# Three-part bf16 maxima, scores without block-diagonal keys, and one exponential per gated unit in a four-layer decoder kernel

## The chip, the cores and the metric

The kernel runs on one core of a Trainium2 chip. The metric is the device time of one launch in microseconds (us). A core has these engines: TensorE (PE) for matmuls, VectorE (DVE), ScalarE (ACT), GpSimd (POOL), and SyncE (SP), which here only starts DMAs. Each engine runs its own instructions in program order, and semaphores join them. Matmuls write to PSUM, 8 banks of 128 x 512 f32; all else lies in SBUF, 128 partitions.

## The reference

Input x is 8 samples x 128 tokens x 128 features, with a context of the same shape. Four decoder layers follow, each of self-attention, cross-attention and a feed-forward part, each part followed by a residual sum and a layer norm. What the change touches:

```python
# L0x: keys and values of the context and of x, causal over x; 16 heads of 8
xc = concat(mem, x); q = x @ Wq; k, v = split(xc @ Wkv)
out = softmax(mask(q k^T * 8**-0.5)) v @ Wout + bout
# L1x: 16 heads of 64 over the context;  L2x: 16 heads of 8 over the context
# L3a: latent attention, rank 64, 16 heads, causal
# L3x: gated (mLSTM) stage, 8 heads of 16
cs = cumsum(log_sigmoid(f)); log_D = where(causal, cs[s] - cs[t] + i[t], -inf)
m = max_t(log_D); D = exp(log_D - m)
C = (q k^T / sqrt(16)) * D
out = C / (max(|sum_t C|, exp(-m)) + 1e-6) @ v
```

## The kernel before

Samples go in pairs (NS = 2 samples, T = 128 tokens each). Two streams, a and b, each take two pairs one after the other (a *turn* each), and every stage of a stream (L0a, L0x, L0f, L1a, L1x, L1f, L2a, L2x, L2f, L3a, L3x) is a Python generator for each engine. `TURN_ORDER` says for each engine how many steps of a and of b come next, so the streams interleave in an order fixed by hand; a stream has a ring of four PSUM banks.

An attention stage does this for each sample u (a *unit*; 8 units for a pair: two each in L0x, L1x, L2x, L3a). PE makes scores with the query token on the partition (`scores8`, `scores64`), in four banks of 4 heads. DVE takes each row's maximum over the keys (L1184; in L0x L1192 for each of two blocks and L1197 to join them) into `m_wide`, f32, 4 of each 32 columns. PE transposes it (`turn_maxima`, L479), and DVE copies the result to `mT` (`pick_maxima`, L1202). Then PE makes the scores again, transposed (`scores8_t`, L507; `scores_t`, L798 and L982), adds a causal mask (L510, L984, a bf16 identity matmul), and subtracts each head's maximum by a matmul of a constant `pick` column, broadcast, with `mT` (`less_maximum`, L492), 16 a unit and block. ACT takes one exponential of 512 columns a bank (L1743), and PE multiplies by the values (L525, L834).

Heads of 8 features sit four to a group of 32 rows. PE can work on tiles of 32 or 64 rows side by side. To take one head's product out of such a group, one side is spread to a block-diagonal form by DVE (`spread_heads`, L1177): `bd_c` (context keys), `bd_k` (own keys), `bd_q` (queries). The first scores use spread keys and `qT`, the transposed scores `bd_q` and keys.

In L3x, `units(first, second)` makes for two of four units (i = 2u + half) the scores (L1041), the mask (L1045) and the cumulated gates (L1050, `pick` with row 5 of `gates`). The other part of log D, row 2 of `gates`, is transposed (L1073), copied by ACT (L1987) and given as the bias of four exponentials a unit, one for each head (L1995). DVE multiplies (L1594). ACT makes the block-diagonal `bd_c` of x (L1974) at the start of the stage.

## Time and profile before

| | |
|---|---|
| median of 3 runs | 1021.25 us (1021.25 to 1021.33) |
| profiled execution, its own time | 1022.06 us |
| span in its profile | 1020.0 us |
| mean granted TensorE clock | 0.952 of full speed |
| PE, matmuls | 904.2 us busy, 89% |
| PE, weight loads (beside matmuls) | 700.2 us, 69% |
| DVE | 539.7 us, 53% |
| ACT | 450.7 us, 44% |
| POOL | 50.8 us, 5% |

The times come from runs without a profile, the busy times from one profiled execution. An f32 matmul of the program is two MATMUL records in the trace, each with a weight load; a bf16 one is one record. A record's duration holds some latency, so for the pace of matmuls the starts of successive groups are compared.

### The profile page before, as it was taken

Reading aid. Unit: us, or ns where it says so; the run is one execution under the profiler, and the core shown is the slowest. Engines: PE = TensorE matmul, PEld = TensorE weight load, DVE = VectorE, ACT = ScalarE, POOL = GpSimd, SP = SyncE. Lnnn points to the kernel's source line nnn. Section 1 sums busy time; section 2 is a strip of 40 time slices with the busy share of each in tenths; the row PEclk is TensorE's granted clock in tenths of the full one; section 3 lists DMA queues with packets and bytes.
Section 4 is the critical chain, followed back from the end, with each engine's and each line's share of the span. In section 5 each row is a group of like instructions: output and inputs, shape, how many; then the busy total and the mean of one; then the engine's idle time right before and its main releaser. Section 6 shows DMA issues by size and latency. Waiting matters only on the chain. (4 is left out here: it accounts for less than half of the span.)

```text
span 1020.0 us, 22561 instructions
## 1 busy us (share of the span) xinstructions
PE 904.2 (89%) x9368; PEld 700.2 (69%) x9368; DVE 539.7 (53%) x1569; ACT 450.7 (44%) x923; POOL 50.8 (5%) x71
## 2 busy tenths in 40 slices
PE   7689899999989998997987979989998989899772
PEld 5257768778778785666556757867887868686441
DVE  5733565653265575347636853655325547454345
ACT  2044343453454673574255233244465446433442
POOL 2300000010010000001000000001001000000000
PEclk8799989999999998999999999999999999999965
DMA  9100000401000301103000000040000030000000
GB/s 344 40 2 3 1 1 1 166 2 37 2 19 1 141 3 40 43 12 139 2 12 1 2 1 2 2 166 33 6 1 19 1 140 1 2 1 2 2 1 21
DMA packets 6838, 36.12 MB, mean 35 GB/s; under 512 B 721, under 2 KB 4305, under 8 KB 5458
## 3 DMA queue, kind: packets, MB, share of 16 engines
q1 hardware_dynamic: 6738, 34.68, 9.1%
q8 instruction: 76, 1.25, 0.5%
q14 instruction: 24, 0.20, 0.1%
HBM read 34.15 MB, written 0.52 MB: 34 GB/s over the span
## 5 line engine op out<-in xcount | busy, mean ns | idle before, releaser
L673 PE MATMUL bank<-xT,weights_F 128*128 128x256 f32 x832 | 202.9, 386 | 3.1 <-ACT p L1818 2.6
L673 PEld LDWEIGHTS bank<-xT,weights_F 128*128 128x128 f32 x832 | 152.0, 193 | 26.8 <-issue 4.2
L681 PEld LDWEIGHTS bank<-weights_F,p 128*128 128x128 f32 x1088 | 133.4, 191 | 18.8 <-DVE p L1363 7.2
L681 PE MATMUL bank<-weights_F,p 128*128 128x128 f32 x1088 | 141.3, 278 | 3.7 <-DVE p L1363 3.0
L1743 ACT ACTIVATE p<-bank 128x512 f32<-128x512 f32 x160 | 84.5, 601 | 121.0 <-PE bank L492 120.9
L1683 ACT ACT_TABLE_LOAD x76 | 97.5, 1283 | 12.9 <-DMA weights_con<-in_con 5.9
L1347 DVE SCALAR_TENSOR_TENSOR res<-bank,comb,res 128x128 f32<-128x128 f32 x184 | 55.7, 345 | 74.1 <-PE bank L681 71.6
L1184 DVE TENSOR_REDUCE m_wide<-bank 128x4 f32<-128x512 f32 x96 | 60.3, 684 | 43.4 <-PE bank L780 33.5
L1818 ACT ACTIVATE p<-bank 128x512 f32<-128x512 f32 x72 | 42.5, 597 | 91.6 <-PE bank L673 91.2
L1363 DVE TENSOR_TENSOR p<-p,bank 128x512 f32<-128x512 f32 x72 | 49.3, 685 | 47.5 <-PE bank L673 27.3
L1894 ACT ACTIVATE p<-bank 128x512 f32<-128x512 f32 x64 | 36.6, 598 | 51.3 <-PE bank L673 51.2
L492 PEld LDWEIGHTS bank<-mT,weights_con 32*128 32x128 f32 x1280 | 46.4, 194 | 17.4 <-issue 13.5
L492 PE MATMUL bank<-mT,weights_con 32*128 32x128 f32 x1280 | 55.1, 296 | 0.0
L1715 ACT ACTIVATE lnv<-mv,weights_con 128x2 f32<-128x2 f32 x56 | 16.6, 296 | 74.7 <-DVE mv L1139 72.7
L1192 DVE TENSOR_REDUCE mx<-bank 128x4 f32<-128x512 f32 x64 | 40.2, 682 | 16.5 <-PE bank L488 16.4
L2037 POOL TENSOR_TENSOR xb<-x_tok,biases 128x256 f32<-128x256 f32 x24 | 19.3, 806 | 575.1 <-DVE x_tok L1147 561.5
L525 PE MATMUL bank<-p,vz 128*32 128x128 f32 x1280 | 42.7, 280 | 4.5 <-ACT p L1743 4.4
L525 PEld LDWEIGHTS bank<-p,vz 128*32 128x32 f32 x1280 | 35.2, 112 | 11.0 <-issue 8.4
L525 PE MATMUL bank<-p,weights_con 128*32 128x128 f32 x1280 | 41.7, 275 | 0.0
L1207 DVE TENSOR_TENSOR attnT<-bank,res 128x128 f32<-128x128 f32 x32 | 9.3, 289 | 55.7 <-ACT res L1748 55.7
L525 PEld LDWEIGHTS bank<-p,weights_con 128*32 128x32 f32 x1280 | 35.9, 111 | 1.0
L1147 DVE TENSOR_SCALAR x_tok<-res,mv,rstd 128x128 f32<-128x128 f32 x88 | 26.4, 343 | 18.1 <-ACT rstd L1716 17.6
(319 smaller groups left out, 1356.0 us busy)
## 6 DMA issues: line engine op xcount, KB each, us to landing
weights_F<-in_L1f SPq DMA_DIRECT2D x2, 4096.0 KB, 13.8
weights_F<-in_L0f SPq DMA_DIRECT2D x2, 3456.0 KB, 13.4
weights_F<-in_L2f SPq DMA_DIRECT2D x2, 3456.0 KB, 12.1
weights_Y<-in_L1x_kv SPq DMA_DIRECT2D x2, 1024.0 KB, 10.6
weights_Z<-in_L1x SPq DMA_DIRECT2D x2, 1024.0 KB, 12.9
weights_Y<-in_L2a SPq DMA_DIRECT2D x2, 898.0 KB, 4.4
weights_Z<-in_L2x SPq DMA_DIRECT2D x2, 449.0 KB, 3.2
weights_L3m<-in_L3m SPq DMA_DIRECT2D x2, 288.0 KB, 6.1
```

The lines of the kernel that those rows point to most:

```text
L492: return mm(b[:, j * T:j * T + T], const("pick")[rows32(i), j:j + 1].to_broadcast([32, P]), s.mT[rows32(i), u], start=False, stop=last)
L525: m = mm(b[rows32(g_), cols], w, probs(g_, i), start=n == 0 and i == 0 and not (part and floor is not None), stop=n == len(blocks) - 1 and ...
L673: m = mm(b[:, k * NT:(k + 1) * NT], W[weight][:, f:f + P], s.xT[:], start=True, stop=True)
L681: m = mm(b[:, tk(u)], h[:, tk(u)], w, start=k == 0, stop=k == len(chunks) - 1)
L1184: o.count(dve.tensor_reduce(s.m_wide[:, u, 32 * i:32 * i + 4], heads(b[:], 4), X, ALU.max), free(st, "s", u, 0, i))
L1192: o.count(dve.tensor_reduce(s.mx[:, u, blk, 4 * i:4 * i + 4], heads(b[:], 4), X, ALU.max), free(st, "s", u, blk, i))
L1347: dve.scalar_tensor_tensor(r, y, s.comb[:, u, e:e + 1], r if i else s.x_tok[:, u], ALU.mult, ALU.add))
L1363: o.count(dve.tensor_tensor(s.p[:, 2 + e % 3], s.p[:, e % 2], bank(st, "up", e)[:], ALU.mult), free(st, "up", e))
L1683: act.preload_act_table_set(functions)
L1743: o.count(act.activation(s.p[:, first + i], b[:], ACT.Exp, scale=scale), free(st, "t", u, blk, i))
L1818: o.count(act.activation(s.p[:, e % 2], b[:], ACT.Silu), free(st, "gate", e))
L1894: o.count(act.activation(s.p[:, 2 * (e % 3) + half], b[:], ACT.Gelu_apprx_tanh), free("L1f", f"up{half}", e))
```

## The change

1. *Maxima in bf16.* After the four maxima of a unit, DVE splits them (`split_maxima`): copy to bf16, remainder, remainder to bf16, remainder of that, so that 12 of each 32 columns of `m_wide` hold three parts. `mT` becomes bf16, and the `pick` matmuls become bf16 with a column that sums three rows. In L1x the parts lie so that a matmul takes 64 rows (`pick64`), as the scores next to it do.
2. *No block-diagonal keys.* `scores8` uses `bd_q` (one head's columns as weights) with `keysT`, in 16 matmuls of 128 columns for 4 of 512. `bd_c` and `bd_k` and their spreads go; the spread of the queries comes before the first scores.
3. *Mask first* in `scores8_t` and in L3a's `scores_t`.
4. *L3x.* The block-diagonal form is made of the context, by POOL in L3a. Row 2 of `gates` is added by PE: a matmul with row 2 as weights and a constant `choose` column, broadcast, behind each `pick` matmul. ACT takes one exponential of 512 columns a unit.
5. *New orders* in `TURN_ORDER` for all engines.

```diff
 TURN_ORDER = {
     "pe":
-        "a1 b1 a2 b1 a2 b1 a2 b3 a1 b1 a1 b1 a1 b2 a1 b2 a3 b1 a2 b1 a1 b2 a1 b1 a1 b2 a1 b1 a1 b1 a2 b1 a6 b1 "
+        "a1 b1 a2 b1 a2 b1 a2 b3 a1 b1 a1 b3 a2 b2 a2 b1 a1 b1 a2 b1 a1 b1 a1 b1 a2 b2 a1 b1 a2 b1 a21 b1 a3 b1 "
...
+    pick_bf = sb("pick_bf", [P, 12], BF16)
-            self.mT = own("mT", NS, T)
+            self.mT = sb(f"mT_{g}", [P, NS, T], BF16)
+            self.m_part = sb(f"m_part_{g}", [P, 2, H], BF16)
...
                 def turn_maxima(st, u):
-                    if st == "L0x":
-                        pe.wait_ge(*told("maxima"))
-                    else:
-                        pe.wait_ge(*freed(st, "s", u, 0, 3))
+                    pe.wait_ge(*told("maxima"))
...
-                def scores8(st, u, keys, mask=None, blk=0):
+                def scores8(st, u, keysT, mask=None, blk=0):
-                    for i, b in enumerate(banks):
-                        filled(mm(heads(b[:], 4), s.qT[rows32(i), tk(u)], keys[rows32(i), u], start=mask is None, stop=True),
-                               st, "s", u, blk, i)
+                    for j in range(4):
+                        for i, b in enumerate(banks):
+                            m = mm(b[:, j * T:j * T + T], s.bd_q[rows32(i), u, j], keysT[rows32(i), tk(u)], start=mask is None,
+                                   stop=mask is None or j == 3)
+                            if j == 3:
+                                filled(m, st, "s", u, blk, i)
...
-                    return mm(b[:, j * T:j * T + T], const("pick")[rows32(i), j:j + 1].to_broadcast([32, P]), s.mT[rows32(i), u],
+                    return mm(b[:, j * T:j * T + T], pick_bf[rows32(i), j:j + 1].to_broadcast([32, P]), s.mT[rows32(i), u],
...
                 def scores8_t(st, u, keysT, mask=None, blk=0):
-                    for i, b in enumerate(banks):
-                        mm(heads(b[:], 4), keysT[rows32(i), tk(u)], s.bd_q[rows32(i), u], start=True, stop=False)
                     if mask is not None:
                         for b in banks:
-                            mm(heads(b[:], 4), ident_bf[:], among(mask, 4), start=False, stop=False)
+                            mm(heads(b[:], 4), ident_bf[:], among(mask, 4), start=True, stop=False)
+                    for i, b in enumerate(banks):
+                        mm(heads(b[:], 4), keysT[rows32(i), tk(u)], s.bd_q[rows32(i), u], start=mask is None, stop=False)
...
                             for n, b in enumerate(banks):
-                                m = less_maximum(u, n, b, j, True)
+                                r, at = n % 2, 4 * (n // 2) + j
+                                m = mm(b[:, j * T:j * T + T], pick_bf[rows64(r), 4 + at:5 + at].to_broadcast([64, P]),
+                                       s.mT[rows64(r), u], start=False, stop=True)
...
                             for j in range(4):
                                 h = 4 * half + j
-                                m = mm(b[:, j * T:j * T + T], const("pick")[rows32(u), h:h + 1].to_broadcast([32, P]),
-                                       s.gates[rows32(u), 5], start=False, stop=j == 3)
+                                mm(b[:, j * T:j * T + T], const("pick")[rows32(u), h:h + 1].to_broadcast([32, P]),
+                                   s.gates[rows32(u), 5], start=False, stop=False)
+                                m = mm(b[:, j * T:j * T + T], s.gates[rows32(u), 2], const("choose")[rows32(u), h:h + 1].to_broadcast([32, P]),
+                                       start=False, stop=j == 3)
...
+                def split_maxima(u):
+                    part = lambda k: heads(s.m_wide[:, u], 4)[:, :, 4 * k:4 * k + 4]
+                    done = o.count(dve.tensor_copy(heads(s.m_part[:, 0], 4), part(0)))
+                    yield
+                    dve.wait_ge(*done)
+                    done = o.count(dve.tensor_tensor(part(1), part(0), heads(s.m_part[:, 0], 4), ALU.subtract))
+                    yield
+                    dve.wait_ge(*done)
+                    done = o.count(dve.tensor_copy(heads(s.m_part[:, 1], 4), part(1)))
+                    yield
+                    dve.wait_ge(*done)
+                    o.count(dve.tensor_tensor(part(2), part(1), heads(s.m_part[:, 1], 4), ALU.subtract), sem("maxima"))
...
-                        for j in range(4):
-                            cols = slice(j * T, j * T + T)
-                            h = 40 + 4 * (i % 2) + j
-                            o.count(act.activation(s.p[:, i, cols], b[:, cols], ACT.Exp, bias=s.small[:, i // 2, h:h + 1]),
-                                    free("L3x", "D", i) if j == 3 else None)
+                        o.count(act.activation(s.p[:, i], b[:], ACT.Exp), free("L3x", "D", i))
...
                 def L3a():
+                    for u in range(NS):
+                        o.count(pool.tensor_tensor(s.bd_c[:, u], among(s.ctxT[:, tk(u)], 4), over(const("head16in64"), T), ALU.mult),
+                                sem("L3x_bd"))
```

On PE, in stream a's first L1x stage, the end of the first sample's transposed scores and the start of the second's stand so before (L798 the scores, L492 the maxima, between them stream b's L1a; the size is partitions x columns of the result, and each row is a group of program matmuls):

```order
L798 MATMUL bank<-wide 128x128 x4
L492 MATMUL bank<-mT,weights_con 128x128 x4
L441 MATMUL bank<-weights_con,x_tok 128x128 x2
L715 MATMUL bank<-xT,weights_L1a 32x128 x2
L719 MATMUL bank<-weights_L1a,xT 128x256 x2
L464 MATMUL bank<-weights_L1a,xT 128x128 x2
L798 MATMUL bank<-wide 128x128 x4
L492 MATMUL bank<-mT,weights_con 128x128 x4
```

and so in the changed kernel, where L800 are the same scores and L805 the maxima:

```order
L800 MATMUL bank<-wide 128x128 x4
L805 MATMUL bank<-mT,pick_bf 128x128 x4
L446 MATMUL bank<-weights_con,x_tok 128x128 x2
L717 MATMUL bank<-xT,weights_L1a 32x128 x2
L721 MATMUL bank<-weights_L1a,xT 128x256 x2
L469 MATMUL bank<-weights_L1a,xT 128x128 x2
L800 MATMUL bank<-wide 128x128 x4
L805 MATMUL bank<-mT,pick_bf 128x128 x4
```

Nothing moved here; what changed is the type and the 64 rows of L805's operands, which the sizes do not show, so that four matmuls of each kind still alternate.

On DVE, the first maxima of stream a's and b's first L0x stage, before (L1192 the maxima of a block, L1197 their join, L1177 the spreads, L1202 the copy of the transpose):

```order
L1192 TENSOR_REDUCE mx<-bank 128x4 x4
L1197 TENSOR_TENSOR m_wide<-mx 128x4x4
L1177 TENSOR_TENSOR wide<-wide,weights_con 128x512 x2
L1202 COPY mT<-bank 128x128
L1177 TENSOR_TENSOR wide<-qk,weights_con 128x512 x2
L1192 TENSOR_REDUCE mx<-bank 128x4 x4
L1172 COPY vz<-bank 128x16x8 x2
L1177 TENSOR_TENSOR wide<-qk,weights_con 128x512 x2
```

and changed (L1216, L1221, L1183 and L1229 are the same operations, L1188 to L1197 the split):

```order
L1216 TENSOR_REDUCE mx<-bank 128x4 x4
L1221 TENSOR_TENSOR m_wide<-mx 128x4x4
L1188 CAST m_part<-m_wide 128x16
L1191 TENSOR_TENSOR m_wide<-m_wide,m_part 128x4x4
L1194 CAST m_part<-m_wide 128x16
L1197 TENSOR_TENSOR m_wide<-m_wide,m_part 128x4x4
L1178 COPY vz<-bank 128x16x8 x2
L1229 CAST mT<-bank 128x128
L1183 TENSOR_TENSOR wide<-qk,weights_con 128x512 x2
```

Before, the transpose could follow L1197 at once and the spreads stood between; now four small operations stand before the transpose, and the spreads of the queries (L1183) come ahead of the scores.

On PE, stream a's last L3x stage, before (L1073 the transposes of `gates`, L1041 scores, L1045 mask, L1050 `pick`; L458, L1026 and L441 are stream b's, which ends its L3a):

```order
L1073 MATMUL bank<-weights_con,wide 128x64 x2
L1041 MATMUL bank<-wide,ctxT 128x512 x2
L1045 MATMUL bank<-neg_causal_t_bf,ident_bf 128x512 x2
L1050 MATMUL bank<-wide,weights_con 128x128 x8
L458 MATMUL bank<-weights_L3a,attnT 128x128 x2
L1026 MATMUL bank<-ctxT,weights_L3x 32x128 x4
L441 MATMUL bank<-weights_con,x_tok 128x128 x2
```

and changed (L463 and L1030 are stream b's L458 and L1026, L1080 the transpose, L1046 scores, L1051 mask, L1056 `pick`, L1058 `choose`):

```order
L463 MATMUL bank<-weights_L3a,attnT 128x128 x2
L1030 MATMUL bank<-ctxT,weights_L3x 32x128 x4
L1080 MATMUL bank<-weights_con,wide 128x64
L1046 MATMUL bank<-xT,wide 128x128 x8
L1051 MATMUL bank<-neg_causal_t_bf,ident_bf 128x512 x2
L1056 MATMUL bank<-wide,weights_con 128x128
L1058 MATMUL bank<-weights_con,wide 128x128
```

The scores are eight matmuls for two, and the last two rows come eight times in a call, one `choose` behind each `pick`; stream b's `project`, which stood behind the call, is ahead of it.

## Rows read from the trace of the kernel before

**Rows 1.** the page, part 1: busy us, share of the span, instructions

```profile
span 1020.0 us, 22561 instructions
PE 904.2 (89%) x9368; PEld 700.2 (69%) x9368; DVE 539.7 (53%) x1569; ACT 450.7 (44%) x923; POOL 50.8 (5%) x71
```

**Rows 2.** three stretches, PE alone: length, busy (count), granted clock, DMA share, GB/s

```profile
110.00:380.00 270.00, 254.85 (x2448) 0.99 0.09 35
380.00:620.00 240.00, 208.98 (x2451) 0.96 0.07 27
950.00:1020.00 70.00, 39.75 (x382) 0.69 0.03 9
```

**Rows 3.** PE's waits: us in total, times, longest us

```profile
PE bank L479 <- DVE m_wide L1197: 3.3, 3, 1.6
PE bank L507 <- DVE mT L1202: 3.8, 5, 1.7
PE bank L488 <- DVE mT L1202: 2.4, 3, 1.5
PE bank L982 <- DVE mT L1202: 1.4, 3, 0.5
```

**Rows 4.** timeline of PE, 96 to 100 us: start us, us, what, [idle before]

```profile
96.49 1.14 PE L507 MATMUL bank<-wide,qk 32*128 32x512 f32 x8
97.56 1.04 PE L510 MATMUL bank<-neg_causal_t_bf,ident_bf 128*128 128x512 bf16 x4
98.53 1.17 PE L492 MATMUL bank<-mT,weights_con 32*128 32x128 f32 x32
99.64 1.16 PE L681 MATMUL bank<-weights_F,p 128*128 128x128 f32 x8
```

**Rows 5.** timeline of PE, 567 to 570 us

```profile
567.26 1.89 PE L673 MATMUL bank<-xT,weights_F 128*128 128x256 f32 x8
568.99 1.03 PE L486 MATMUL bank<-neg_causal_bf,ident_bf 128*128 128x512 bf16 x4
569.95 1.13 PE L488 MATMUL bank<-wide,qk 32*128 32x512 f32 x7
```

**Rows 6.** timeline of PE, one sample of an L1x unit

```profile
190.62 0.71 PE L798 MATMUL bank<-wide 64*128 64x128 f32 x8
191.26 0.50 PE L492 MATMUL bank<-mT,weights_con 32*128 32x128 f32 x8
191.69 0.72 PE L798 MATMUL bank<-wide 64*128 64x128 f32 x8
...
194.93 0.27 PE L726 MATMUL bank<-weights_con,wide 64*128 64x64 f32 x1
```

**Rows 7.** timeline of PE in stage L3x, 450 us

```profile
450.35 1.71 PE L1050 MATMUL bank<-wide,weights_con 32*128 32x128 f32 x16
451.98 1.16 PE L681 MATMUL bank<-weights_F,p 128*128 128x128 f32 x8
```

**Rows 8.** timeline of PE, router logits with 8 moving columns

```profile
299.95 0.51 PE L666 MATMUL bank<-weights_small,xT 128*128 128x8 f32 x4
300.31 1.54 PE L673 MATMUL bank<-xT,weights_F 128*128 128x256 f32 x6
```

**Rows 9.** timeline of DVE, 998 us: small operations that each wait for the last

```profile
998.19 0.17 DVE L1609 TENSOR_SCALAR small<-small 128x16 f32<-128x16 f32 x1
998.39 0.25 DVE L1610 RECIPROCAL small<-small 128x16 f32<-128x16 f32 x1
```

**Rows 10.** groups of DVE by form: busy us, mean ns

```profile
L1177 DVE TENSOR_TENSOR wide<-qk,weights_con 128x512 f32<-128x512 f32 x32 | 22.1, 730 | 0.0
```

**Rows 11.** groups of POOL by form

```profile
L2066 POOL TENSOR_TENSOR x_all<-weights_L3m 128x512 f32<-128x512 f32 x1 | 1.3, 1260 | 0.0
```

**Rows 12.** groups of ACT by form

```profile
L1743 ACT ACTIVATE p<-bank 128x512 f32<-128x512 f32 x160 | 84.5, 601 | 121.0 <-PE bank L492 120.9
L1995 ACT ACTIVATE p<-bank,small 128x128 f32<-128x128 f32 x64 | 17.4, 382 | 18.8 <-PE bank L1050 18.8
```

More of the change, by code:

```diff
@@ L50 @@
                ("ones", 128), ("spread", 128), ("tiny16", 128), ("feats", 64), ("head8in32", 4), ("head16in64", 4),
-               ("pick", 8), ("cos", 8), ("sin", 8), ("eps", 5)]:
+               ("pick", 8), ("choose", 8), ("pick3", 4), ("pick64", 8), ("cos", 8), ("sin", 8), ("eps", 5)]:
     CONST[_n] = (_at, _w)
@@ L531, in probs_at, with softmax8 @@
                     return lambda g_, i: s.p[:, first + g_, i * T:i * T + T]
-                def softmax8(st, keys, keysT):
-                    scores8(st, 0, keys)
+                def softmax8(st, keysT):
+                    pe.wait_ge(*told("queries", NS))
+                    scores8(st, 0, keysT)
                     yield
@@ L945, in L2x @@
                     pe.wait_ge(*freed("L2x", "q"))
-                    pe.wait_ge(*told("L2x_keys", NS))
-                    yield from softmax8("L2x", s.bd_k, s.kT)
+                    pe.wait_ge(*freed("L2x", "k"))
+                    yield from softmax8("L2x", s.kT)
                     project("L2x", W["L2x_o"])
@@ L1071, in L3x @@
                     pe.wait_ge(*told("L3x_gates"))
-                    for k, row in enumerate((4, 2)):
-                        m = tr(b[:, 64 * k:64 * k + 64], s.gates[:, row], IDENT[0:64, 0:64])
-                    filled(m, "L3x", "mx")
+                    filled(tr(b[:, 0:64], s.gates[:, 4], IDENT[0:64, 0:64]), "L3x", "mx")
                     yield
-                    pe.wait_ge(*told("L3x_bd"))
+                    pe.wait_ge(*told("L3x_bd", NS))
                     units(0, 3)
@@ L1183, in maxima @@
                         b = bank(st, "s", u, 0, i)
-                        o.count(dve.tensor_reduce(s.m_wide[:, u, 32 * i:32 * i + 4], heads(b[:], 4), X, ALU.max),
+                        at = 32 * (2 * (i % 2) + i // 2 if st == "L1x" else i)
+                        o.count(dve.tensor_reduce(s.m_wide[:, u, at:at + 4], heads(b[:], 4), X, ALU.max),
                                 free(st, "s", u, 0, i))
+                    yield
+                    dve.wait_ge(*freed(st, "s", u, 0, 3))
+                    yield from split_maxima(u)
                 def block_maxima(st, u, blk):
@@ L1214, in softmax @@
                     yield
-                    if queries is not None:
-                        spread_heads(s.bd_q, queries, sem("queries"))
-                        yield
                     yield from maxima(st, 1)
@@ L1261, in L0a @@
                         dve.wait_ge(*told("kept"))
-                    def context_keys():
-                        dve.wait_ge(*freed("L0x", "kc"))
-                        spread_heads(s.bd_c, s.kcT, sem("L0x_ctx_keys"))
-                    yield from tail("L0a", s.x_in, context_keys)
+                    yield from tail("L0a", s.x_in)
                 def L0x():
@@ L1546, in L2x @@
                     dve.wait_ge(*freed("L2x", "q"))
+                    spread_heads(s.bd_q, s.qT, sem("queries"))
                     yield
-                    yield from softmax("L2x", s.qT)
+                    yield from softmax("L2x")
                     for u in range(NS):
@@ L1971, in L3x @@
                     exp_ln()
-                    act.wait_ge(*ring.freed((pair, "L3a", "xT")))
-                    for j in range(4):
-                        o.count(act.activation(s.bd_c[:, :, j], by_sample(s.xT[:]), ACT.Identity,
-                                               scale=const("head16in64")[:, j:j + 1]), sem("L3x_bd") if j == 3 else None)
-                    yield
                     act.wait_ge(*told("L3x_absf"))
@@ L1984, in L3x @@
                     b = bank("L3x", "mx")
-                    per_head = lambda k: b[:, 64 * k:64 * k + 64].rearrange("p (u h) -> p u h", u=NS)[:, :, 0:HC]
-                    o.count(act.activation(s.small[:, :, 32:40], per_head(0), ACT.Exp, scale=-1.0))
-                    link(act.copy(s.small[:, :, 40:48], per_head(1)), free("L3x", "mx"))
+                    per_head = b[:, 0:64].rearrange("p (u h) -> p u h", u=NS)[:, :, 0:HC]
+                    o.count(act.activation(s.small[:, :, 32:40], per_head, ACT.Exp, scale=-1.0), free("L3x", "mx"))
                     yield
```

69 lines of the change are left out of this document (35 added, 34 removed), and 55 rows, old and new, of the table TURN_ORDER.

## The prediction, before the changed kernel was run

> **What bounds the kernel now.** I read the page's part 1 first: TensorE (PE) is busy 904.2 of 1020.0 us, DVE and ACT about half of it, POOL 5% [rows 1]. So PE work is the first suspect, and the question is where it is gap-free. The windows answer that [rows 2]. From 110 to 380 us, where one stream is in an expert stage (L0f, L1f) and the other in L1a or L1x, PE is busy 254.85 of 270 us, 94%. From 380 to 620 us, where the streams pass through L3a, L3x, L0a and L0x, it is 209 of 240 us, 87%. In the last 70 us it is 40. PE time taken out of the first stretch (and of its twin in the second turn) should come off the end nearly whole; in the second, part of it turns into waiting; in the last, a chain of waits rules and not PE's work. The waits show what would be late there: PE waits for the maxima, as DVE makes them (L1197) or copies them (mT, L1202), 14 times in four rows, for 10.9 us [rows 3], out of 32 units (8 for each of 4 pairs) that go through such a chain.
>
> **How PE's time is made up.** An end is modelled, so I take starts. An f32 matmul is two records. Eight records of 256 columns start 1.73 us before the next group, 0.216 each, 0.84 ns a column; four bf16 records of 512 columns take 0.96 us, or 0.86 without one change of tile shape, 0.42 ns a column [rows 5]. So f32 costs four bf16 passes. Thirty-two records of 32 rows run on four row groups at a time: 8 x 128 x 0.84 = 0.86 us, and the row says 1.11 to the next group; the same for 4 x 512 columns is 1.07 [rows 4]. The 0.2 to 0.25 over is what a change of tile shape costs. L1x shows it best: 8 records of 64 rows take 0.65 us before 32-row ones start, where 4 x 128 x 0.84 = 0.43 is streaming, and those take 0.43 where 0.215 is [rows 6]. Each change costs 0.22 us, and a unit has eight: 194.93 - 190.62 = 4.31 us.
>
> **The change on PE.**
> (a) *bf16 maxima outside L1x.* There are 40 groups of 16 maxima matmuls, 8 of them in L1x. For the other 32, 16 bf16 matmuls on four row groups stream for 4 x 128 x 0.42 = 0.215 us instead of 0.86, with the shape change kept: -0.65 us each, -20.8 us. Bounds: the load of weights may set the pace instead. Four f32 records with 8 moving columns take 0.36 us [rows 8], 0.09 each, so a load alone can take as long as 107 ns of f32 streaming. If a bf16 load is no faster, four row groups side by side give 4 x 0.107 = 0.43 us, and the gain is 13.9. I take the streaming value, since four f32 pairs of load and matmul already pass in 0.107 us here, with half of these loads gone in bf16.
> (b) *L1x, maxima as 64-row tiles.* The alternation stays, but the shape no longer changes: 4 x (0.43 + 0.107) + one change = 2.36 us for 4.31, -1.95 x 8 = -15.6 us. With loads at 0.107: 4 x (0.43 + 0.215) + 0.22 = 2.8, -12.1. If f32 to bf16 on one shape cost as a shape change does, it would be -3.4; but [rows 5] has f32 to bf16 at 128 rows with 1.73 for 8 x 0.216, so nothing is paid there.
> (c) *Mask first in L0x's transposed scores.* 32, 128, 32 rows becomes 128, 32, 32: one change less in 8 groups, -1.8. In L3a it is 128, 64, 32 for 64, 128, 32: nothing.
> (d) *Scores against kT, 16 x 128 columns for 4 x 512 in 24 groups.* Same columns; 1.11 for 1.07 [rows 4], +1.0. L3x's scores likewise keep their columns, and rotate over the same two row groups: 0.
> (e) *L3x, the bias by PE.* A call of units() has 8 pick matmuls, the four of a unit on one row group, so nothing runs beside them: 451.98 - 450.35 = 1.63 us [rows 7]. The change puts a choose matmul of the same size and row group behind each: +1.63 x 8 = +13.1 us at full clock, twice that at half. Gone are 4 small transposes, -0.4.
> Sum on PE: -20.8 - 15.6 - 1.8 + 1.0 + 13.1 - 0.4 = -24.5 us.
>
> **The change elsewhere.** DVE: four small operations for each of 32 units, each waiting for the one before, at 0.20 us from start to start [rows 9]: 0.8 us longer from the last reduction to the transpose, +26 us of DVE in all. In return 24 spreads (L1177) go, 0.73 us each [rows 10], -17.5. DVE's total hardly moves, and half of it is idle. What is queued behind the four on DVE is the other stream's work; who waits for them is PE at its next transpose. With the 14 waits above and 0.8 us each, the most that is exposed is 11 us as the waits now stand; against it the spreads of keys in L0x go. I take +3 (four units). The first scores of L0x and L2x used to start from qT itself; now they wait for the spread of the queries, two operations or 1.5 us later, and PE's queue behind them with them: eight such places, 12 us if nothing covered them. What covers them is the other stream's matmuls, which stand ahead of the scores in PE's order; I take +2. ACT: in L3x four exponentials of 128 columns, 2.18 us a call for 8, become one of 512 a unit, 0.60 [rows 12]: -1.0 us a call. That shortens the chain in the last 70 us by two to four calls, and the doubled PE work, there partly at 1.2 for 2.4 GHz (0.69 granted, [rows 2]), lengthens it by as much; I set the two against each other. POOL makes the block-diagonal context, two operations of 128x512 a pair at about 1.26 us [rows 11], at the start of L3a for reads in L3x; without that cover a pair would wait 2.5 us. ACT gets two more table loads in the new order (82 for 80); it is not the bound, 0.
> The part of (a) in stages with 87% cover (24 groups, 15.6 us) I count at 85%: +2.4.
> Sum: -24.5 + 3 + 2 + 2.4 = **-17 us**. The profiled execution took 1022.06 (span 1020.0 and 2 around it), the median is 1021.25; I expect about 1005 profiled and **1004 us** median, 1000 to 1008 with small errors of the terms.
>
> Of loads, the Trainium skill ("TensorE: Matmul & The Clock Gate", LDWEIGHTS) says that a load takes its columns over 1.2 GHz, 107 ns for 128, whatever the rows; its section on weight-path modes says that non-f32 weights of 128 columns load about twice as fast. [Rows 8] has 0.09 us a load and agrees roughly for f32. By the first rule alone (a) and (b) would be the lower values, by the second the upper ones.
>
> **Rivals.**
> *Loads set the pace:* -13.9 - 12.1 - 1.8 + 1.0 + 13.1 - 0.4 + 7.4 = -7, 1014 us. For it: [rows 8]. Against: half as many loads per matmul. 0.15.
> *The split maxima bind (slower):* the four operations are queued in order on DVE, and a 0.7 us reduction of the other stream can stand between any two. If each of the 32 units is exposed for the 0.8 us and one such operation, 1.5 us, that is 48 us against 24.5: 1021 + 24 = 1045. It decides from 24.5/32 = 0.77 us a unit on. Against it: only 14 of 32 units are waited for now, and in the 94% stretches PE has expert matmuls in between. At its threshold it is a draw, a little above it 1025 to 1030. 0.07; the draw itself, within 0.2%, 0.03.
> *The clock falls more often:* the granted clock is 0.96 from 380 to 620 us and 0.99 from 110 to 380 [rows 2]; a share 1 - c of lost clock costs at most that share of the stretch, 9.6 and 2.7 us, 15 over the kernel. If lighter PE groups doubled it: 1019. 0.07. The same page of the Trainium skill (HAM oscillation) ties half clock to idle stretches; by it, L3x with doubled matmuls would rather gain clock, as its PE queue has fewer gaps.
> *The new orders also close waits:* PE's idle time is 116 us [rows 1]; 31 of it stand between 380 and 620 us, 17 more than 94% cover would leave [rows 2]. If the orders take 10 to 15 of these: 989 to 994. 0.18.
> My forecast: 0.50.
>
> **Range and chances.** Low end 988, by the last rival; high end 1014, by the load rival. The slower rival, the draw and the clock's stay out (0.17), with what lies under 988. Faster by over 0.2% (what a measurement of this kernel tells from no change) 0.90, within 0.2% 0.03, slower 0.07.
>
> **What would show it.** (1) Maxima groups: half the records; 0.46 us to the next group where the shape changes (0.68 if loads pace). (2) An L1x unit 2.4 us for 4.3. (3) L3x: 3.3 us a call at full clock. (4) PE busy near 880; idle near 116 to 125. (5) PE waits for the last of the four small operations, in fewer than 20 of 32 units. The prediction is wrong if PE's busy time falls as said and its idle time takes it back, or if the matmuls of (1) and (2) don't get shorter.

## The result and the profile after

| | us, median | range, runs | ratio to before, 95% interval |
|---|---|---|---|
| before | 1021.25 | 1019.62 to 1026.75, 6 | |
| changed | 1048.61 | 1043.46 to 1051.67, 6 | 1.0254 [1.0219, 1.0288] |

The changed kernel is 27 us slower, where 17 us faster was forecast. The page of its profiled execution (1047.02 us, span 1045.0) begins so; it answers to [rows 1]:

```profile
span 1045.0 us, 22918 instructions
PE 908.7 (87%) x9524; PEld 725.5 (69%) x9524; DVE 550.3 (53%) x1674; ACT 439.9 (42%) x857; POOL 55.5 (5%) x79
```

PE's busy time did not fall to 880 but rose by 4.5, and its idle time rose from 115.9 to 136.3. Yet the products that the change makes cheaper became so. The timeline of PE in the changed kernel at the maxima of one unit, and in L1x (one sample of a unit), answers to [rows 4] and [rows 6]:

```profile
419.77 0.39 PE L497 MATMUL bank<-mT,pick_bf 32*128 32x128 bf16 x16
...
190.80 0.71 PE L800 MATMUL bank<-wide 64*128 64x128 f32 x8
191.34 0.28 PE L805 MATMUL bank<-mT,pick_bf 64*128 64x128 bf16 x4
191.46 0.67 PE L800 MATMUL bank<-wide 64*128 64x128 f32 x8
191.96 0.28 PE L805 MATMUL bank<-mT,pick_bf 64*128 64x128 bf16 x4
192.07 0.67 PE L800 MATMUL bank<-wide 64*128 64x128 f32 x8
```

Sixteen bf16 records are 0.39 us from first start to last end. The next group starts 0.33 us after the first start in 11 of the 25 such groups at the full clock, and 0.36 in the middle one (1.10 before). In L1x eight f32 records and four bf16 ones take 0.50 + 0.12 us, and the changes of shape between them are gone: 4 x 0.62 = 2.5 us a unit for 4.31.

Where the time went shows once PE's busy time is parted by clock. In the trace's records TensorE has either its full clock (2.4 GHz, granted 1.00) or half of it (1.2 GHz, 0.50). I add three terms to the span: *work*, PE's busy time with what lies in half-clock stretches counted half; *idle*; and *lost*, the other half of the busy time in these stretches. They are worked out from the trace's matmul and clock records, and are good to some 5 us (kernels with the same products differ by up to that, e1 and the changed one by 8). Each row is one execution, and the runs of a kernel differ: the rows of e2, e6 and e8 are of runs 3 to 4 us under their median, those of e5, e12, e11, e4, e9, e18 and e13 of runs 3 to 10 us above it.

```
profiled executions, us             span    work   idle   lost   half clock in all
before                            1020.0   867.3  115.9   36.8    98.6
changed                           1045.0   847.4  136.3   61.3   154.7
e1  changed, orders of before     1038.3   855.6  133.5   49.2   126.0
e2  maxima with the split         1013.4   837.6  135.9   39.8   109.4
e12 the same, nobody waits        1014.5   834.1  128.4   52.0   132.7
e7  maxima without the split       992.4   834.2  120.2   37.9   102.2
e3  scores from spread queries    1030.3   870.0  120.8   39.5   105.6
e8  the same, wait by unit        1015.9   870.4  117.3   28.2    81.7
e4  L3x                           1042.3   880.0  111.4   50.9   134.3
e5  L3x, the spread alone         1021.2   874.7  114.1   32.4    95.5
e6  L3x, row groups in turns      1019.1   872.9  113.1   33.1    90.2
e9  e7 + masks + e8 + e6          1007.9   833.4  120.7   53.9   137.2
e10 changed + e6's and e8's mends 1028.5   836.2  137.8   54.5   141.5
e11 e10 without the split         1017.2   834.5  132.8   49.8   125.7
e13 e9 without L3x                1007.4   832.3  122.5   52.6   132.7
e14 e9 without scores and masks    998.3   833.3  119.3   45.6   117.5
e15 e7, picks of L3x in turns      994.6   829.6  122.9   42.2   112.9
e16 e10, waits for the split filled 1015.6 851.6  132.7   31.2    84.2
e17 e15, waits for x_tok filled    993.7   844.0  117.8   31.9    89.1
e18 e17, waits for maxima too     1002.3   852.7  113.8   35.7    95.5
```

So the change took 20 us of work from PE, and gave back 20 in idle time and 24.5 at the half clock. Both are seen in the windows of PE alone (length, busy, granted clock, DMA share, GB/s) and its timeline in the changed kernel around 409 us:

```profile
403.00:409.00 6.00, 3.45 (x45) 1.00 0.01 3
409.00:419.20 10.20, 9.22 (x66) 0.50 0.01 2
979.00:1013.00 34.00, 33.08 (x198) 0.50 0.00 1
```

```profile
404.12 2.06 PE L782 MATMUL bank<-qk,wide 64*128 64x128 f32 x32
408.73 0.30 PE L481 MATMUL bank<-weights_con,m_wide 128*128 128x128 f32 x1 [2.55 <-DVE m_wide L1197]
409.53 2.09 PE L515 MATMUL bank<-wide,qk 32*128 32x512 f32 x8 [0.50 <-DVE mT L1229]
```

PE stands 2.55 us for the last of the split's operations, and from 409.0 to 419.2 it is 9.22 of 10.20 us busy at half the clock. If the stall is what brought the half clock, it cost its 2.55 us and then some 4.6 more. DVE's timeline there shows what PE waited for, the last reductions of the unit and then the four links (operations that each wait for the one before), which are 0.8 of the 2.55 us:

```profile
405.99 1.89 DVE L1205 TENSOR_REDUCE m_wide<-bank 128x4 f32<-128x512 f32 x3 [0.29 <-PE bank L782]
407.79 0.17 DVE L1188 CAST m_part<-m_wide 128x16 bf16<-128x16 f32 x1
407.99 0.17 DVE L1191 TENSOR_TENSOR m_wide<-m_wide,m_part 128x16 f32<-128x16 f32 x1
408.20 0.17 DVE L1194 CAST m_part<-m_wide 128x16 bf16<-128x16 f32 x1
408.40 0.18 DVE L1197 TENSOR_TENSOR m_wide<-m_wide,m_part 128x16 f32<-128x16 f32 x1
408.50 0.68 DVE L1205 TENSOR_REDUCE m_wide<-bank 128x4 f32<-128x512 f32 x1
```

Links follow each other at 0.20 us, as forecast. PE's waits in the changed kernel (total, times, longest) answer to [rows 3]:

```profile
PE bank L481 <- DVE m_wide L1197: 14.1, 8, 2.6
PE bank L491 <- issue: 7.3, 5, 2.5
PE bank L530 <- ACT p L1760: 7.2, 8, 1.7
PE bank L515 <- DVE mT L1229: 2.4, 5, 0.5
```

The transposes' wait is 14.1 us in 8 places. It was 4.2 in 5: to the 3.3 in 3 of [rows 3] comes a row of the kernel before for the other stages,

```profile
PE bank L479 <- DVE m_wide L1184: 0.9, 2, 0.5
```

More waits came beside it: the first scores (L491), which now need the spread queries, wait 7.3 us at their start ("issue": the profile names no releaser), and the values (L530) wait 7.2 for exponentials, for 4.4 before.

The window from 979 to 1013 us shows something else: PE busy 33.08 of 34 us, nearly without a gap, and yet at half the clock. The timeline of PE there, in a call of units() of L3x:

```profile
981.60 1.04 PE L1051 MATMUL bank<-neg_causal_t_bf,ident_bf 128*128 128x512 bf16 x2
982.57 0.79 PE L1056 MATMUL bank<-wide,weights_con 32*128 32x128 f32 x2
983.15 0.63 PE L1058 MATMUL bank<-weights_con,wide 32*128 32x128 f32 x2
983.58 0.63 PE L1056 MATMUL bank<-wide,weights_con 32*128 32x128 f32 x2
...
989.00 0.69 PE L446 MATMUL bank<-weights_con,x_tok 128*128 128x128 f32 x2
```

From 982.57 until the next group at 989.00 the call takes 6.4 us; three of the last four calls run so, where at the full clock a call takes 3.4 (1.64 in the kernel before, [rows 7]).

### The profile page after: what moved, and what is told of

It is laid out like the page before. It is cut to its first block and busy times, and to the rows that moved or that the text cites. A ratio compares the mean times of both kernels' runs of the same rounds, so it can differ in the third digit from the quotient of the medians.

```text
span 1045.0 us, 22918 instructions
## 1 busy us (share of the span) xinstructions
PE 908.7 (87%) x9524; PEld 725.5 (69%) x9524; DVE 550.3 (53%) x1674; ACT 439.9 (42%) x857; POOL 55.5 (5%) x79
## 5 line engine op out<-in xcount | busy, mean ns | idle before, releaser
L530 PE MATMUL bank<-p,vz 128*32 128x128 f32 x1280 | 46.0, 292 | 8.5 <-ACT p L1760 7.2
L1216 DVE TENSOR_REDUCE mx<-bank 128x4 f32<-128x512 f32 x64 | 40.1, 683 | 22.9 <-PE bank L491 22.9
L1911 ACT ACTIVATE p<-bank 128x512 f32<-128x512 f32 x64 | 36.8, 597 | 35.2 <-PE bank L675 34.9
L530 PEld LDWEIGHTS bank<-p,vz 128*32 128x32 f32 x1280 | 38.1, 118 | 15.9 <-issue 12.2
L530 PE MATMUL bank<-p,weights_con 128*32 128x128 f32 x1280 | 42.9, 278 | 0.0
L530 PEld LDWEIGHTS bank<-p,weights_con 128*32 128x32 f32 x1280 | 36.7, 112 | 1.0
L1739 ACT COPY xT<-bank 128x256 f32<-128x256 f32 x40 | 15.0, 375 | 42.6 <-PE bank L446 42.6
L1764 ACT ACTIVATE res<-bank 128x128 f32<-128x128 f32 x32 | 8.9, 279 | 52.1 <-PE bank L530 52.0
## 6 DMA issues: line engine op xcount, KB each, us to landing
weights_F<-in_L1f SPq DMA_DIRECT2D x2, 4096.0 KB, 12.7
weights_F<-in_L2f SPq DMA_DIRECT2D x2, 3456.0 KB, 11.3
```

The lines of the kernel that those rows point to most:

```text
L530: m = mm(b[rows32(g_), cols], w, probs(g_, i), start=n == 0 and i == 0 and not (part and floor is not None), stop=n == len(blocks) - 1 and ...
L1216: o.count(dve.tensor_reduce(s.mx[:, u, blk, 4 * i:4 * i + 4], heads(b[:], 4), X, ALU.max), free(st, "s", u, blk, i))
L1911: o.count(act.activation(s.p[:, 2 * (e % 3) + half], b[:], ACT.Gelu_apprx_tanh), free("L1f", f"up{half}", e))
```

## Experiments

All but e1, e10, e11 and e16 start from the kernel before, in its orders. Medians are set against runs of the kernel before on the same chip (1021.3 to 1022.4). Below each expectation stand the median in us, the range, and the ratio to before with its 95% interval. The masks first (part 3 of the change) were not run alone.

### Part by part

**e1_old_orders.** All new code, `TURN_ORDER` of before (the split's four operations in one step, since the old order has no places for them).

> All four changes of the code with the orders of before (the split of a unit's maxima is one step with its last maximum, the removed steps stand empty). If the new orders lose the time: 1000 to 1005 us, as was predicted. If the code itself does, by the gates added on PE in L3x or by the wait for the split maxima: 1035 to 1055 us.

1040.08 (1039.18 to 1041.8), 1.0177 [1.0156, 1.0199]. The code is slow by itself; the new orders, with the split in steps of its own, add some 8 us.

**e2_maxima_only.** Maxima in three bf16 parts with the split, and L1x's 64-row tiles:

```diff
+                    pe.wait_ge(*told("maxima"))
...
-  const("pick")[rows32(i), j:j + 1].to_broadcast([32, P]), s.mT[rows32(i), u]
+  pick_bf[rows32(i), j:j + 1].to_broadcast([32, P]), s.mT[rows32(i), u]
...
+                    split_maxima(u)
```

> The kernel before with the bf16 maxima and their split alone, old orders. PE loses about 36 us of work. If PE's work sets the end and the split is hidden: 988 to 995 us. If PE waits for the split in most of 32 units, and loses clock behind these waits: 1010 to 1030 us. If the loss of the change lies in L3x or in the orders, this one is well below 1021.

1019.62 (1014.96 to 1025.0), 0.9971 [0.9949, 0.9994]. PE's work falls by 29.7 us and the time by 2.5, as expected for the case that PE waits for the split and loses clock behind it. PE's waits:

```profile
PE bank L482 <- DVE m_wide L1193: 19.4, 19, 2.9
PE bank L447 <- DVE x_tok L1152: 17.2, 15, 7.6
```

Nineteen of 32 transposes wait, for 19.4 us (4.2 us in 5 places before).

**e3_scores_only.** Scores as `bd_q` against kT, 16 products of 128 columns; no spread keys; PE waits for both units' queries.

> The kernel before with the scores of L0x and L2x taken against keys as they are, from spread queries, alone. By the prediction's terms +1 on PE and +2 of waits less 17 us of DVE work: 1020 to 1024 us. If the scores that wait for the queries' spread are what costs: 1026 to 1035 us.

1031.15 (1027.22 to 1037.0), 1.0087 [1.0052, 1.0121]: +9. A wait of 7.2 us in 6 places stands ahead of the scores that the kernel before does not have.

**e4_L3x_only.** The context spread by POOL, the choose products, one exponential per unit.

> The kernel before with L3x's changes alone (context spread by POOL, choose matmuls on PE, one exponential a unit). By the prediction 13 us of PE, half covered: 1028 to 1035 us. If the doubled matmuls of one row group run at half clock and sit on the chain of the last stage: 1040 to 1050 us. If the shorter exponentials pay for them: 1019 to 1023 us.

1039.05 (1033.47 to 1046.13), 1.0153 [1.0086, 1.022]: +17. But the four runs are of two kinds: 1033.5 and 1033.8 us at a mean granted clock of 0.949, and 1044.3 (the profiled one) and 1046.1 at 0.936, where the kernel before has 0.948 to 0.953. In the first kind L3x costs 11.5 us, in the second 23. In the profiled run work is +12.7 as forecast, idle -4.5, lost at the half clock +14.1, and three of the last four calls run at the half clock, 6.4 us each for 3.4.

### Each part's cause

**e5_L3x_spread_only.** e4 without the choose products; ACT keeps four exponentials.

> The kernel before with one third of the change to L3x: GpSimd spreads the retrieved context over the heads and the transposed scores are sixteen 128x128 products; no choose products, and ScalarE keeps its four biased exponentials per unit. All of the L3x change together cost +17 us (e4). Theory A (the choose products are the cost: they double the f32 work of one row group, and in the last turns they run at the half clock): this kernel stays within 4 us of the kernel before, 1018 to 1026, and the last L3x calls take 1.5 to 2.9 us each. Theory B (the spread on GpSimd comes late, or the small products cost more than the wide ones): 1030 or more with PE waiting ahead of the L3x calls.

1020.18 (1013.09 to 1023.27), 0.9974 [0.9948, 0.9999]. Theory A: the choose products are the cost, since the spread by POOL and the small scores cost nothing.

**e6_L3x_interleaved.** e4 with neighbours on PE in different row groups:

```diff
-  for i, b in zip(both, banks):
-      for j in range(4):
-          mm(... pick, rows32(u) ...); mm(... choose, rows32(u) ...)
+  for j in range(4):
+      for i, b in zip(both, banks): mm(... pick, rows32(i // 2) ...)
+      for i, b in zip(both, banks): mm(... choose, rows32(i // 2) ...)
```

> The whole change to L3x on the kernel before, as e4 (1039), but the pick and choose products of the two units of a call take turns, so that neighbours on PE lie in different 32-row groups. Theory A (one row group at a time is what makes the products long, and two groups overlap): a call falls from 3.2 us to some 1.7 to 2.2 us at the full clock and the time to 1026 to 1032. Theory B (the two groups' products write the same kind of bank and PE takes an f32 product at its own rate whatever its rows): a call stays at 3.2 us, 1036 to 1042. Theory C (the clock alone matters): calls stay at 3.2 us but the last stretch is at the full clock, 1028 to 1034.

1024.06 (1018.93 to 1026.45), 1.0001 [0.9982, 1.0021]: 15 us better than e4, with the same products, and 2 us better than theory A said. At the same granted clock of 0.949 it is 1024 for e4's 1033.6, so some 10 of the 15 us come with the order of the products and the rest with the clock that two of e4's runs had lost. Groups of PE by form in e4, then in e6 (busy us, mean ns):

```profile
L1056 PE MATMUL bank<-wide,weights_con 32*128 32x128 f32 x128 | 28.6, 340 | 0.0
L1058 PE MATMUL bank<-weights_con,wide 32*128 32x128 f32 x128 | 27.6, 325 | 0.0
```

```profile
L1055 PE MATMUL bank<-wide,weights_con 32*128 32x128 f32 x128 | 14.3, 301 | 0.0
L1059 PE MATMUL bank<-weights_con,wide 32*128 32x128 f32 x128 | 13.4, 288 | 0.0
```

The busy time halves. A part of that is the clock, which three calls of e4 had at half; at the full clock a call is 2.0 us, to the next group, for 3.4, since two products now overlap. The Trainium skill ("TensorE: Matmul & The Clock Gate", Part 3: Packing small matmuls) has small products run side by side when they lie in different row groups; this case agrees. PE's timeline in e6's last turn:

```profile
981.78 0.49 PE L1055 MATMUL bank<-wide,weights_con 32*128 32x128 f32 x4
982.11 0.39 PE L1059 MATMUL bank<-weights_con,wide 32*128 32x128 f32 x4
982.33 0.39 PE L1055 MATMUL bank<-wide,weights_con 32*128 32x128 f32 x4
```

Three of its last four calls run at this pace, where in the changed kernel and in e4 three of four ran at half the clock. Whether the order of the products brings the clock too is taken up at e11.

**e7_one_part_maxima.** e2 without the split. The maximum subtracted is the one rounded to bf16; numerator and denominator have the same, so it divides out.

> As e2 (bf16 maxima, 64-row tiles in L1x, orders and all else of the kernel before), but without the split: the maximum that is subtracted is the one rounded to bf16, which divides out of the softmax, and the transpose waits for the maxima as in the kernel before. PE has the same products as e2 (rows 4 to 11 of each 12 are zero). Theory A (the four operations of the split between the maxima and the transpose took back what PE saved: +16 us of waits in e2): PE waits for the maxima fall from 19 to some 4 us and the time to 998 to 1008. Theory B (PE's saved time is lost whatever the split does, because VectorE and ScalarE or the chain through the two streams set the pace): 1015 to 1022, with the idle time moved to other waits.

996.23 (994.43 to 999.22), 0.9744 [0.9707, 0.9781]: theory A, 23 us below e2 with the same products on PE. The transposes' waits are 7.1 us for 19.4:

```profile
PE bank L485 <- DVE m_wide L1206: 5.1, 4, 1.8
PE bank L485 <- DVE m_wide L1193: 2.0, 3, 1.1
```

**e8_queries_by_unit.** e3, with `told("queries", 1)` ahead of each unit's scores for `told("queries", NS)` ahead of the first.

> As e3 (scores from spread queries, no spread keys; 1031), but PE waits ahead of each unit's scores for that unit's spread alone, not for both. Theory A (the wait for the queries' spread, which is now right behind the last projection, is what cost +9 us): half of each wait goes, 1024 to 1029. Theory B (the form of the products, sixteen of 128 columns against four of 512, or the moved spreads on VectorE, cost it): 1030 to 1032 as e3.

1021.2 (1017.07 to 1026.39), 0.9981 [0.9957, 1.0005]: 10 us below e3, and 3 below the range of theory A. The wait itself fell only from 7.2 to 4.1 us. Of the 14.4 us between the profiles, 11.3 are in *lost*, 3.5 in *idle*; and the granted clock is higher in every run, 0.953 to 0.961 for 0.942 to 0.952.

**e12_split_nobody_waits.** e7 with the split's four operations done into a tile that nothing reads.

> As e2 (1020) and e7 (996): VectorE does the four operations of the split, but into a tile that nothing reads, and the transpose waits for the maxima alone, as in e7. Theory A (what costs is PE's wait for the split at the transpose): 996 to 1004. Theory B (what costs is VectorE's 14 us of more work, which makes all its later results late): 1012 to 1020, with PE waiting for the scores' maxima or the transposed maxima instead.

1012.96 (1004.0 to 1016.51), 0.9902 [0.9868, 0.9937]. The transposes wait as in e7, 6.9 us in 7 places:

```profile
PE bank L486 <- DVE m_wide L1220: 4.9, 4, 1.9
PE bank L486 <- DVE m_wide L1205: 2.0, 3, 1.1
```

So it is mostly theory B: of the 23 us between e2 and e7, waiting for the split at the transpose is 7, and 17 come with DVE's operations though nobody waits for them. Some of DVE's later results come late (waits for the copied maxima 6.3 us at L514 for 3.8 in e7). In the profile 8 us of the difference to e7 are idle time and 14 are lost at the half clock; the granted clock was 0.935 to 0.947 in its five runs, for 0.945 to 0.949 in e7's four.

### The mends together, and the orders

**e9_all_mended.**

> The candidate: one-part bf16 maxima without the split (e7), masks first in the transposed scores, scores from spread queries with a wait per unit (e8), and the whole L3x change with the two units' row groups taking turns (e6), in the orders of the kernel before. Against before e7 was -25.7 us, e8 -2 and e6 0. If the parts add (theory A) it takes 992 to 998 us; if they share the same idle time (theory B: with less PE work the waits on VectorE's layer norms and maxima bind), 996 to 1004 with PE idle above 135 us.

1004.13 (991.22 to 1009.95), 0.9795 [0.9752, 0.9839], its profiled run the slowest of them. The median is at the upper edge of theory B, but PE's idle time is 120.7 us, not above 135, so neither theory holds: work and idle are e7's, and 16 us more are lost at the half clock in that run.

**e10_after_mended_split_kept.** The changed kernel in its own orders with e6's and e8's edits.

> The changed kernel with its own orders and its split, but with the row groups taking turns in L3x and the queries' wait per unit. The two mends took 15 and 10 us from the single-part kernels (e4 to e6, e3 to e8). Theory A (the same two places cost the same in the changed kernel): 1021 to 1028. Theory B (the half clock and the new orders are the larger part, and the places only carried them): 1035 or more.

1030.25 (1025.28 to 1032.34), 1.008 [1.0053, 1.0108]: 18 us off the changed kernel's time, near theory A (2 us above its bound).

**e11_after_mended_no_split.**

> As e10, and the split's four operations left out (its steps stay as empty places in the order; the subtracted maximum is the rounded one, which divides out). Theory A (the split is a chain between the maxima and the transpose, worth 23 us on the old orders): 998 to 1006, with PE waits for the maxima under 6 us. If the new orders cost some 8 us whatever else (theory B), it ends 6 to 10 us above e9; if they only hurt because of the waits (theory C), within 3 us of e9.

1014.86 (1004.83 to 1020.87), 0.9866 [0.983, 0.9902]: 15 us better than e10, and 9 above the range of theory A. It is 11 above e9, which differs in the orders (and in where the split's places were). That is near theory B, that the new orders cost about as much here as between e1 and the changed kernel, but the runs of both kernels spread by more than 11 us.

This run also bears on the gap-free stretch at half the clock. Its products take turns between the row groups, as in e6 and e10. Three windows of PE, the first of e11 and two of e10, where the stretch begins as in the changed kernel, at 979 us:

```profile
959.70:987.00 27.30, 26.48 (x211) 0.50 0.01 1
```

```profile
979.10:982.50 3.40, 3.40 (x26) 0.50 0.02 5
982.50:985.90 3.40, 2.33 (x38) 1.00 0.00 0
```

e10 has the full clock back after 3.4 us. e11, with the same products in the same turns, is 26.48 of 27.30 us busy and stays at the half clock throughout; three of its last four calls take 3.7 us for 2.0. So alternating the row groups does not by itself bring the full clock back, and one row group at a time is not needed for a gap-free stretch at half the clock.

**e13_one_part_scores_masks** and **e14_one_part_L3x_interleaved** take e9 apart.

> e9 without the L3x change: one-part maxima, masks first, scores from spread queries with a wait per unit. e7 alone took 996, e9 1004 (991 to 1010). Theory A (the masks or the scores bring the half clock that e9 showed in the middle): 1001 to 1008 with over 60 us of the half clock between 60 and 950. Theory B (the L3x change brings it): 992 to 998.

> e9 without the scores and the masks: one-part maxima and the L3x change with the row groups taking turns. Theory A of e13: 994 to 999, as e7, since L3x in turns cost nothing on the kernel before (e6). Theory B of e13: 1002 to 1008.

999.78 (995.29 to 1009.42), 0.9795 [0.9752, 0.9838], and 998.21 (991.7 to 1000.44), 0.9757 [0.9724, 0.9789]. The first lies between its two theories, the second in theory A; the intervals overlap. Neither part helps e7, and which one brings the half clock stays open.

**e15_one_part_pick_in_turns.**

> e7 with one more edit: in the kernel before's L3x the sixteen f32 products of a call (one per head, all of a unit in one 32-row group one after the other) alternate between the two units' row groups. If two row groups overlap, as e6 showed for 32 of them, a call falls from 1.5 to 0.8 us at the full clock, and the two calls of the last turn, at the half clock, from 2.7 and 2.7 to some 1.4: 991 to 996. If it is nothing: 994 to 999 as e7.

994.79 (988.7 to 1003.23), 0.9732 [0.9692, 0.9772]. A call (eight products, sixteen records) takes 1.1 us to the next group for 1.64; the time does not differ from e7's by what can be told.

### Filling PE's waits

**e16_waits_filled.** e10 with PE given something to do ahead of each transpose's wait:

```diff
                     b = opened("dve", st, "mT", u)
+                    for _ in range(2):
+                        mm(heads(b[:], 4), ident_bf[:], among(neg_causal_bf[:], 4), start=True, stop=True)
                     pe.wait_ge(*told("maxima"))
```

> e10 (the changed kernel with both mends and its split, 1030) with two more products of 128x512 bf16, some 0.43 us at the full clock, ahead of each of the 32 waits for the split, into the transpose's own bank, which the transpose then overwrites: 13.7 us of idle work, of which the waits cover what they can. Theory A (idle stretches of PE bring the half clock): the half clock between 60 and 950 falls well below e10's 83 us and the time stays within 1026 to 1034 in spite of the work. Theory B (idle time does not bring it): half clock as e10, time 1036 to 1044.

1019.5 (1014.14 to 1023.11), 0.9975 [0.9957, 0.9993]: 11 us faster than e10 with 15 us more work. Theory A, and beyond its bound. The granted clock was 0.952 to 0.965 in all ten runs, for 0.927 to 0.939 in e10's four. PE from 60 to 950 us in e10, then in e16:

```profile
60.00:950.00 890.00, 795.02 (x8441) 0.95 0.08 29
```

```profile
60.00:950.00 890.00, 798.12 (x8613) 0.98 0.08 29
```

Over the whole span idle fell by 5 us and lost by 23, and the transposes' waits from 14.3 us to 8.6. So what PE does at these places decides over much of the half clock in the changed kernel; it is not only that waits and half clock occur together. The products stand at all 32 places, of which 9 waited in e10, so this run does not part the filled waits from the added work.

**e17_norm_waits_filled** (two such products ahead of each wait for x_tok, in e15) and **e18_both_waits_filled** (one more ahead of the maxima's).

> e15 (one-part maxima, L3x products in turns; 995, PE 123 us idle, 42 us lost at the half clock) with two products of 128x512 bf16 that nobody reads ahead of each wait for the layer norm's output (36 or so places, 15 us at the full clock), in the bank that the transposes then overwrite. Theory A (filling PE's waits keeps the clock): idle falls by 8 to 12 us, the loss at the half clock by 10 or more, and the time is 984 to 993. Theory B (what e16 gained is special to the split's waits): the added work lengthens it, 998 to 1006.

> e17 with one such product more ahead of each of the 32 waits for the maxima (7 us at the full clock). Here those waits are short, with the split gone (5 us in all). Theory A: no further gain, since there is little to fill: 0 to 6 us above e17. If the half clock falls further still, at most 4 us below e17.

995.72 (995.36 to 999.58), 0.9745 [0.9716, 0.9774], and 995.47 (995.14 to 1004.28), 0.9743 [0.9713, 0.9773]. In e17 work +14, idle -5, lost -10: a draw, where theory A had 984 to 993 and theory B 998 to 1006. Filling paid at the split's waits and not at these.

## Why the prediction was wrong

**Right.** (a) and (b), the shorter maxima: -36.4 forecast, -33 of work in e7 (and 0.33 to 0.36 us to the next group, under the 0.46 forecast and well under the 0.68 of the loads' rival, which is out). (b)'s unit 2.5 us for 2.36. (e)'s products: +13.1 - 0.4 forecast, +12.7 of work in e4, 3.4 us a call to the next group, as forecast within 0.1. (d)'s form: +1.0 forecast, +2.7 to +3.1 of work in e3 and e8. Of PE's sum, -24.5, the changed kernel's profile shows -20. Sign (5) came true as well: 8 of 32 units wait for the last operation of the split. PE busy near 880 did not: 908.7, since the half clock lengthens what is busy.

Forecast and result are 44 us apart. Set side by side, the parts are -31 forecast and -2.5 measured for the maxima, +3 and +9 for the scores, +12.7 and +17 for L3x, nothing and +8 for the orders, and -1.8 for the masks, which no run shows alone.

**Wrong in size: "I take +3 (four units)", waits for the split.** With "+2.4" for cover, maxima alone should have given -31; e2 gives -2.5, and e7, without the split, -25.7. The step that failed is this term: it is 23 us, not 3. The count of exposed units came from the waits as they stood before, when DVE had less to do and PE more; nineteen were exposed in e2. And e12 shows the larger part, 17 us, to be another thing than the term counted: "What is queued behind the four on DVE" was named and given no price.

**Put at nothing: "I set the two against each other", the clock in L3x's last stretch.** The 12.7 us of work came as forecast, and in e4's two runs at a granted clock like before's L3x costs 11.5. In its two other runs it costs 23, and in the profile of the changed kernel, as in e4's, three of the last four calls take 6.4 us for 3.4. These 9 us are "the doubled PE work, there partly at 1.2 for 2.4 GHz", which the sum cancelled against 1.0 us a call saved on ACT. That a product in one row group can have a neighbour beside it when the order allows was in the text ("nothing runs beside them") as a price and not as something that can be changed; e6 takes 15 us back by it, some 10 of them at an equal clock.

**Wrong in size: "I take +2", the queries' spread.** With (d), +3 forecast and +9 measured; waiting by unit (e8) takes all of it away, more by the clock than by the wait itself.

**Not priced: the new orders,** +8 (changed against e1), a rival of 0.18 for the opposite sign.

**The clock.** "If lighter PE groups doubled it: 1019" is the rival nearest in mechanism: the lost time went from 36.8 to 61.3 us, 24.5 more. The prediction put the loss of the kernel before at 15 us, from stretches that had few waits; the table has 36.8, and the 70 us at 0.69 in [rows 2] alone allow up to 22. Doubled from 36.8 the same rival would have stood near 1041. It was also taken as a thing apart, with 0.07. It is not wholly apart: e16 moves 23 us of it with two small products at the split's places. But it follows the idle time by no fixed rate: e2's profile has 20 us more idle than before and 3 more lost, e4's 4.5 less idle and 14 more lost. The parts measured alone sum to -2.5 + 9 + 17 + 8 = 31.5, for 27 together. Beside the clock rows: the Trainium skill ("TensorE: Matmul & The Clock Gate", HAM oscillation) ties the half clock to idle stretches. Between 60 and 950 us e16 agrees (lost 37.2 us in e10, 15.9 in e16). The windows from 979 to 1013 us in the changed kernel and from 959.7 to 987 in e11 do not: 97% busy and half the clock throughout.

**The slower rival,** split maxima bind, 1045, had the direction and nearly the number, but by another sum: 48 us of bare exposure against 24.5, where the changed kernel's profile shows 20 of idle time and 24.5 of clock, and where L3x alone gives +17.

**Open.** Why gap-free stretches near the end keep the half clock. It is not the use of one row group at a time: e11 has such a stretch with the groups in turns. It is not the moment at which the half clock begins either: in e10 it begins at 979.1 us, as in the changed kernel (979.0), and is over at 982.5. Which part of e9 brings its half clock, and why DVE's unwaited operations (e12) do, beyond 8 us of idle time, was not settled either; runs of one kernel spread by up to 19 us (e9) through it.

## What to carry to other kernels

Price a new link in a chain by who gets late behind it, on its engine too, and not by the waits that the old trace shows; leaving the link out (the rounded maximum that divides out) was worth 23 us where making products cheaper behind it was worth 2.5. Small f32 products in one row group cost 1.7 times what they do when neighbours alternate between two groups (3.4 and 2.0 us a call), so order them so before counting. On a PE at 87 to 89% keep three terms apart, work, idle and lost at the half clock, and look at more than one run: 30 us less work was worth 2.5 in e2, where idle rose by 20, and 33 less was worth 25.7 in e7, where idle and lost stayed near. The best kernels here are e7 and e15 (0.974 [0.971, 0.978] and 0.973 [0.969, 0.977]); e14, e17 and e18 are not told from them.

## What the runs showed of the hardware that was not expected

- Adding 15 us of products that nobody reads made a kernel 11 us faster (e10 to e16), through a granted clock of 0.98 for 0.95 between 60 and 950 us.
- PE was 97% busy for 34 us at a granted clock of 0.50 in the changed kernel, with f32 products of 32 rows in one row group among its work, and 97% busy for 27 us at 0.50 in e11, with the same products in two groups in turns.
- f32 products of 32 rows, 128 columns, cost 3.4 us for the 16 of a call in one row group at a time, and 2.0 us in two groups taken in turns, the same change of shape in both.
- Four bf16 products on 64 rows between f32 products on 64 rows take 0.12 us, and the eight f32 records beside them 0.50, where with a change of shape on each side they took 0.65 [rows 6]. Of the 0.43 us that the two changes cost, some 0.07 are left.
